# Softmax denominators of a cross-attention, moved between the two halves of the next score strips

## The reference

```python
def step(params, x):
    z = x @ t_k.T
    y = x @ t_v.T
    grads = jax.grad(loss_fn)(params, z, y)
    new_params = tree_map(lambda p, g: p - LR * g, params, grads)
    return new_params, _recon(new_params, x @ t_q.T)
```

```python
scores = einsum('bqhs,bkhs->bhqk', q, k) / sqrt(HEAD_DIM)
scores = where(context_mask[:, None, None, :], scores, -inf)
attn = softmax(scores, axis=-1)
out = einsum('bhqk,bkhs->bqhs', attn, v).reshape(B, Tx, C)
return out @ Wo.T + bo
```

## Time and profile before

| what | value |
|---|---|
| runs (us) | 739.61, 747.83, 747.27; median 747.27 |
| profiled execution | span 745.8 us, the only time that the page gives for it |
| mean granted TensorE clock | 0.858 of full |
| busy | PE 599.8 us (80%), PEld 479.7, DVE 482.3, ACT 433.1, POOL 366.9 |
| the stage of the change | scan and first cross-attention, from 63 to some 262 us |

### The profile page before, as it was taken

How to read it: one execution, slowest core, us unless ns; L and a number is a source line. 1 busy time by engine, 2 the same in 40 slices (tenths; PEclk the granted TensorE clock), 3 DMA queues, 4 the chain that set the end, 5 groups by cost and what they waited for, 6 DMA issues and landing times.

```text
span 745.8 us, 18652 instructions
## 1 busy us (share of the span) xinstructions
PE 599.8 (80%) x6242; PEld 479.7 (64%) x6242; DVE 482.3 (65%) x1357; ACT 433.1 (58%) x897; POOL 366.9 (49%) x666
## 2 busy tenths in 40 slices
PE   2897999999998823999848999996997972399970
PEld 1485677777776623999725676764665661399970
DVE  7653548856877342555437999986998874355546
ACT  1452368866775203888515667664886651388850
POOL 5711334543678663566642243322466867166650
PEclk9896569977998655999958999999999996599995
DMA  7849960000000011222190000000000001122216
GB/s 198 254 144 320 333 201 2 2 1 3 8 16 20 23 35 47 69 73 74 40 331 38 2 2 2 2 2 2 2 3 13 24 23 46 42 78 70 72 39 167
DMA packets 41854, 52.61 MB, mean 71 GB/s; under 512 B 11056, under 2 KB 36897, under 8 KB 41473
## 3 DMA queue, kind: packets, MB, share of 16 engines
q1 hardware_dynamic: 37217, 42.07, 18.5%
q0 software_dynamic: 4544, 9.35, 3.8%
HBM read 40.97 MB, written 28.22 MB: 93 GB/s over the span
## 4 chain that ended last, share of the span: by engine, by line
PE 44%; DVE 14%; issue 13%; POOL 12%; DMA 2%; ACT 1%; another core or an unknown queue 1%; SPq 1%; POOLq 0%; DVEq 0%; ACTq 0%
POOL yo L1530 10%; PE p_pT L1371 9%; PE p_s L1357 6%; PE p_o L1397 6%; PE p_o L1402 5%; PE p_s L1348 2%; POOL to_row L1525 2%; DVE x_inv L1129 2%; DVE x_prob L1122 2%; DVE x_top L1112 2%; DVE x L1581 2%; PE p_in L1328 2%; PE p_in L1322 1%; PE p_o L1411 1%
## 5 line engine op out<-in xcount | busy, mean ns | idle before, releaser
L1588 ACT ACTIVATE context<-pack 128x1156 f32 x78 | 90.6, 1166 | 48.4 <-DVE table L1214 30.1
L1530 POOL DMA_INDIRECT yo<-context,to_row x78 | 76.1, 976 | 66.2 <-issue 38.7
L1624 PE MATMUL p_s<-xT_f,context 128*128 128x128 f32 x624 | 85.6, 282 | 0.0
L1624 PEld LDWEIGHTS p_s<-xT_f,context 128*128 128x128 f32 x624 | 79.1, 199 | 0.0
L1076 POOL DMA_INDIRECT xs<-send,x_index x64 | 64.1, 1002 | 22.1 <-issue 16.8
L1557 DVE TENSOR_SCALAR context<-p_s,context 128x128 f32<-128x128 f32 x156 | 47.5, 346 | 34.1 <-PE p_s L1624 34.1
L1268 ACT ACTIVATE x_pT<-p_pT 128x512 f32<-128x512 f32 (+1 forms) x96 | 48.9, 525 | 24.7 <-PE p_pT L1371 22.3
L1371 PE MATMUL p_pT<-sq,x_prob 128*128 128x128 f32 x320 | 56.4, 304 | 3.0 <-ACT x_pT L1268 1.6
L1112 DVE TENSOR_REDUCE x_top<-p_s 128x12 f32<-128x924 f32 (+2 forms) x48 | 46.9, 1005 | 10.8 <-PE p_s L1357 10.6
L1595 ACT ACTIVATE context<-p_s,context 128x128 f32<-128x128 f32 x156 | 47.6, 355 | 6.2 <-PE p_s L1624 4.4
L1122 DVE TENSOR_TENSOR x_prob<-p_s,x_top 128x768 f32<-128x768 f32 (+2 forms) x96 | 50.0, 575 | 0.1
(11 more groups left out here) (247 smaller groups left out, 1533.6 us busy)
## 6 DMA issues: line engine op xcount, KB each, us to landing
xs<-in_blank SPq DMA_DIRECT2D x2, 8707.5 KB, 43.2
pack<-in_pack SPq DMA_DIRECT2D x16, 578.0 KB, 8.2
context<-xs SPq DMA_DIRECT2D x78, 64.5 KB
back<-yo SPq DMA_DIRECT2D x16, 256.0 KB, 4.8
yo<-context,to_row POOLq DMA_INDIRECT x78
x<-in_x SPq DMA_DIRECT2D x4, 256.0 KB, 4.5
xs<-send,x_index POOLq DMA_INDIRECT x64
out<-x SPq DMA_DIRECT2D x4, 256.0 KB, 2.3
```

The source lines that it names most:

```text
L1530: nc.gpsimd.indirect_dma_start(yo[:, :], bass.IndirectOffsetOnAxis(to_row[:, n % NY, :], 0), y[:, n % NY, :], None).then_inc(y_stored[n % ...
L1588: nc.scalar.activation(ws[:, n % NW, :], pack[:, bass.ds(e, 1), :].rearrange("p a w -> p (a w)"), ACT.Copy).then_inc(ws_ready, 1)
L1624: ins = mm(p_h[n % 2][k // 2][:, P * (k % 2):P * (k % 2 + 1)], ws[:, n % NW, P * k:P * (k + 1)], xT[:, n % 2, :], start=True, stop=True)
```

## The change

`score` is cut in two: strips 0 and 2 stay in it, strips 3 and 1 become `score_rest`. The second half of `mix`, the 12 products that sum the exponentials, becomes a step `sums` of its own. FIRST_PE runs `sums` with lag 5, so one round after its mixing, between the two parts of the scores. For the attentions of the second layer nothing moves.

```diff
--- before.py
+++ after.py
@@ -110,7 +110,7 @@
 
 
 
-FIRST_PE = ((3, "score"), (0, "aT"), (1, "aq"), (0, "a"), (4, "tp0"), (5, "po"), (0, "eT"), (2, "turn_in"), (1, "gw2"), (4, "tp1"), (1,
+FIRST_PE = ((3, "score"), (5, "sums"), (3, "score_rest"), (0, "aT"), (1, "aq"), (0, "a"), (4, "tp0"), (5, "po"), (0, "eT"), (2, "turn_in"), (1, "gw2"), (4, "tp1"), (1,
     "out"), (0, "e_"), (7, "rturn"), (0, "dh"), (4, "tp2"), (8, "rank"), (2, "project"), (0, "g2"), (0, "g1"), (4, "mix"), (0, "g1b"), (7,
     "rlogit"))
 FIRST_DVE = ((5, "scale"), (8, "choose"), (3, "max"), (0, "eTa"), (5, "res"), (1, "w2n"), (0, "slope2"), (0, "slope3"), (1, "comb"), (0,
@@ -1348,7 +1348,10 @@
                     mm(to, m["ident_bf"][:, :], m["alibi"][:, hs[0]:hs[-1] + 1, :].rearrange("p h k -> p (h k)"), start=True, stop=False)
             pe.wait_ge(q_sb, FIRST + b + 1)
             pe.wait_ge(k_sb, FIRST + b + 1)
-            for g in (0, 2, 3, 1) if beside else range(NG):
+            score_strips(b, p, (0, 2) if beside else range(NG))
+
+        def score_strips(b, p, order):
+            for g in order:
                 r = slice(STRIP * g, STRIP * (g + 1))
                 if beside and g == 1:
 
@@ -1358,7 +1361,11 @@
                               start=False, stop=g in (1, 3) if beside else True)
                 if beside and g in (0, 2):
                     last.then_inc(strips_scored, 1)
-            last.then_inc(scored, 1)
+            if order[-1] in (1, 3):
+                last.then_inc(scored, 1)
+
+        def score_rest(b, p):
+            score_strips(b, p, (3, 1))
 
         def turn_p(groups):
             def run(b, p):
@@ -1395,6 +1402,10 @@
                 for g in range(NG):
                     c, r = of_strip[g][i], slice(STRIP * g, STRIP * (g + 1))
                     mm(po_mix[r, :], values(b, p, i, g), pT[:, c, :], start=i == 0, stop=i == len(of_strip[0]) - 1)
+            if not beside:
+                sums(b, p)
+
+        def sums(b, p):
             for i in range(len(of_strip[0])):
                 for g in range(NG):
                     c, r = of_strip[g][i], slice(STRIP * g, STRIP * (g + 1))
@@ -1447,7 +1458,7 @@
             last.then_inc(ranked, 1)
 
         if beside:
-            return dict(score=score, turn_in=turn_in, project=project, tp0=turn_p((0,)), tp1=turn_p((1,)), tp2=turn_p((2,)), mix=mix, po=project_o,
+            return dict(score=score, turn_in=turn_in, project=project, tp0=turn_p((0,)), tp1=turn_p((1,)), tp2=turn_p((2,)), mix=mix, sums=sums, score_rest=score_rest, po=project_o,
                         rturn=route_turn, rlogit=logits, rank=rank)
         if own:
             return [(2, score), (3, turn_p((0, 1))), (4, project_o), (0, turn_in), (3, turn_p((2, 3))), (0, project), (3, mix)]
```

## The result

| | before | after |
|---|---|---|
| median of 4 runs | 743.44 us (739.40 to 747.83) | 777.07 us (759.79 to 800.83) |
| profiled execution | 745.8 us of span | 784.95 us, span 782.9 |

The four runs of the changed kernel took 759.79, 769.18, 784.95 and 800.83 us at mean granted clocks of 0.827, 0.822, 0.797 and 0.782: the lower the clock, the longer the run. The span of before had 0.858. Here the low clock is the effect of the change itself, so that ratio understates it: by the medians it is 1.045. The prediction was 742.0, from 737 to 751; the result lies outside, on the side of rival D.

The account below looks back on a forecast made before the run. TensorE was taken to bound the stage. The terms, 0 + 0.9 + 1.3 + 0.9 - 8.4 = -5.3 us, took the 745.8 us span to 740.5; with the median 1.5 us above the span, 742.0 us, range 737.0 to 751.0.

Parts of the forecast that it names:

- rival D: Slower: with mixing and sums apart the clock may not rise; 759 us at four such rounds, 767 at six; chance 0.05.
- Term 4: Granted clock: 24 dense passes moved into the thin stretch between strips and scan stop two slow rounds, -8.4 us.
- other direction: Parted mixing and sums: some 3 us more at half clock at first rise, 1 to 2 us, in range only.
- Term 1: Sums between strips, 14 rounds: 0.25 us wait goes, two shape changes cost 0.18; -0.07 to 0 a round, taken as 0.
- Rival C: Each change of array shape around the sums costs more than 0.09 us; +2.9 us in all, 744.9 us; chance 0.08.
- Term 2: VectorE's reciprocal, scale and max come later: 0 in ordinary rounds, +0.9 us in round 12, +1.3 in round 17.
- list of signs: What the trace should show if right, among others the reciprocal 1.1 us behind the masks' start instead of 0.8.
- rival A: Clock falls as before or again elsewhere, perhaps from TensorE's longer idling in round 12: 750.4 or 746.2 us; chance 0.30.
- Term 3: Drain, rounds 19 and 20: sums stand behind the router's logits, 0.45 us twice, +0.9 us.

## Why the prediction was wrong

**The failed step is Term 4 with its "other direction", and rival D, which is what happened.** The text had seen that two rises lay where the sums ran right behind the mixing, priced their parting at one late rise of 1 to 2 us, and gave the case that the clock does not rise 0.05. In its place the clock stayed at half until 154.7 and from 202.5 to 342.4. The mixing twice (33 us faster than the change for 9 us more work) and the count of rows (31 of 38 long ones followed by a rise, 3 of 33 rows of 12) show that the parted row is the cause. The trace of before held more than the two: the third rise, at 182.1, lies in the sums as well (181.32 to g1b at 182.37), and the row at 238.31 was not followed by one. What misled was counting dense passes moved into a thin stretch as if the clock answered to each of them alike. At full clock it stayed up with them; at half clock, apart from the mixing, they did not lift it. The stretch was not as thin as the text has it either: beside its small products stand the strips with 308 columns and the masks with up to 462.

**The price of a half-clock round was too low.** Rival D took 4.2 us from rounds 9 and 11 of before. These were at half clock for 10.2 us only, so the rows said 0.41 us per us at half clock; a round spent wholly there loses 7.0 (measured) and not 4.2. At four to six such rounds D gave 759 to 767; there were eight of them at half clock (5 to 7, 13 to 17), six of them 6.8 to 7.0 us longer than before, round 16 5.0 and round 17, where before was itself partly at half clock, 2.0.

**Term 4's own gain came.** Rounds 8 to 11 ran at full clock, 8.5 us shorter than before; the sum had -8.4. That the filled stretch is what keeps the clock up is not shown: the kernel with the sums ahead of masks and strips, and nothing between the strips, had no fall in these rounds either. It was outweighed by 20.5 + 3.2 + 27.8 + 2.2.

**Term 1 was right:** 9.75 against 9.78 us for a round at full clock, inside -0.07 to 0. The two more changes of shape cost about what the gap of the strips gave back; no run measures the two apart. Rival C would have shown 0.2 us more a round and fell.

**Term 2 was right in size.** It put the reciprocal at 136.55 with the masks at 134.76, 1.79 us behind them; it is 1.76. (The list of signs said 1.1, which forgot that the masks move too.) It stays hidden in ordinary rounds. In round 12 TensorE's stall grew by 0.95 us for a forecast of 0.9. What was missing is the clock: it fell right behind the stall, as rival A feared, and then stayed down, which neither A (3.1 us) nor the sum held. That the stall caused the fall is not shown: it came in round 12 with shorter stalls too. In round 17 the +1.3 did not show, since TensorE at half clock was later than VectorE.

**Term 3, +0.9 us, can't be told** in a drain at half clock: there the logits take 0.53 us ahead of the sums in each of the two rounds, which is its size.

**The chances.** 0.97 on "within 2%" rested on the view that the clock's moves are worth a few us. The range should have held D to its end. The spread of before, 8.2 us, had been put down to one or two slow rounds; it was as well a sign of how much hangs on the clock.

**Still open:** what property of a stretch the clock answers to. The experiments vary the number of like products in a row and do not tell their number from their width or from what stands just behind them. One rise of the change (154.7) came behind a row of 12, so such a row can do it, rarely. Also open is why one execution of a kernel gets the rise and the next does not, and what makes the clock fall in round 12.

## To carry to other kernels

Where a stage is bounded by TensorE and its granted clock changes between 0.5 and 1.0, look first for what runs just before each rise, and don't cut that row apart without a test: here that cost 34 us by the medians, for a wait of 0.25 us a round. Price a lost rise per us at half clock (0.42 us here) times all rounds until the next rise, not by one partly slow round. Work done for nothing can pay: 12 products more in six rounds took 43 us off the change (39 when each is set against its own runs of before), and were 0.5% faster than the kernel before (0.992 to 0.999).

## Not expected of the hardware

- A busy TensorE does not get its full clock by being busy: 66.97 of 67 us at 0.50. Nor does it keep it: before fell at 148.0 and 171.9 in the middle of rounds that it bounds.
- A fall beside a stall of 2.09 us was followed by 140 us at half clock (202.5 to 342.4) in the change, and one beside a stall of 2.10 us by 7 us (182.2 to 189.0) where a doubled row of mixing stood behind it.
- Runs of one kernel spread over 41 us (the change, four runs) or 3 us (extra mixing in six rounds, ten runs). A whole row alone does not make the spread small: with tp0 between the strips it was 41 us as well. Two chips differed by 14.6 us on the kernel before (739.35 and 753.93).
